# Front and projection stages of a four-layer kernel: inputs summed from plain loads, more statistics groups, normalisation moved to ScalarE, input stage reordered

## The reference, cut to what matters

```python
x = hidden_states                                   # (4, 1024, 256)
x = x + mamba(layernorm(x))                         # front + scan
x = x + top2_experts(layernorm(x))
x = x + attention(layernorm(x))                     # projection stage + attention
x = x + expert_choice(layernorm(x))

# mamba, up to its scan
xz = h @ in_proj_w;  x, z = split(xz)               # 256 -> 2 x 512
x = silu(conv4(x) + conv_b)
dt_low, B, C = split(x @ x_proj_w)                  # 64, 16, 16
dt = softplus(dt_low @ dt_proj_w + dt_bias);  du = dt * x

# attention, up to its scores
q = rope((h @ Wqa) @ Wqb);  k, v = split((h @ Wkva) @ Wkvb);  k = rope(k)
```

## Time and profile before

| | us |
|---|---|
| median of three runs | 2639.83 (2638.99 to 2640.31) |
| profiled execution, its own time | 2635.56 |
| span of that execution | 2633.9 |
| front stage | 0 to 235 |
| projection stage | 1381 to 1513 |

### The profile page before, as it was taken

The page is one execution under the profiler, slowest core; times in us unless marked ns, Lnnn a source line. Parts: engine busy times, 40 slices in busy tenths (PEclk is TensorE's granted clock), DMA queues, the critical chain, the costliest instruction groups (busy, mean ns, idle before and its releaser), DMA issues. The chain is left out here.

```text
span 2633.9 us, 35521 instructions
## 1 busy us (share of the span) xinstructions
PE 2274.5 (86%) x11483; PEld 1340.5 (51%) x11485; DVE 1810.7 (69%) x2771; ACT 1325.2 (50%) x2531; POOL 1337.9 (51%) x1000
## 2 busy tenths in 40 slices
PE   7994888989989986499985599999998539999998
PEld 3432444544545544399972334444445326666666
DVE  7997999999999995755544798888884651111200
ACT  4776888787887782022222546666665202111120
POOL 1545999899898891277755512222221012333332
PEclk9996999999999998699996889999999759999999
DMA  4457235124133104544437522112200322333322
GB/s 160 163 187 242 70 130 192 49 77 147 49 108 132 49 17 136 171 72 72 71 54 150 150 37 33 33 33 42 39 3 4 128 89 54 75 80 68 70 54 24
DMA packets 149650, 231.20 MB, mean 88 GB/s; under 512 B 26113, under 2 KB 98881, under 8 KB 149378
## 3 DMA queue, kind: packets, MB, share of 16 engines
q1 hardware_dynamic: 119170, 189.22, 23.2%
q0 software_dynamic: 30336, 40.16, 9.5%
HBM read 151.99 MB, written 81.66 MB: 89 GB/s over the span
## 5 line engine op out<-in xcount | busy, mean ns | idle before, releaser
L1114 POOL TENSOR_TENSOR scan_hC<-scan_h,scan_c_all 128x1024 f32<-128x1024 f32 x256 | 612.4, 2418 | 70.3 <-DVE scan_h L1034 69.2
L1034 DVE TENSOR_TENSOR_SCAN scan_h<-scan_dA,banks 128x1024 f32<-128x1024 f32 x224 | 504.3, 2275 | 22.9 <-ACT scan_dA L987 14.9
L884 PE MATMUL banks<-scan_hC,all_ident 128*128 128x512 f32 x1024 | 486.5, 600 | 26.4 <-DVE scan_xc L1041 26.4
L2200 ACT ACTIVATE attn_pt<-banks 128x1024 f32<-128x1024 f32 (+3 forms) x384 | 292.2, 810 | 186.9 <-PE banks L2147 185.7
L976 ACT ACTIVATE scan_scaled<-scan_duT,scan_bT 128x128 f32<-128x128 f32 x1024 | 312.0, 388 | 15.1 <-PE banks L861 14.7
L987 ACT ACTIVATE scan_dA<-scan_dt,mamba_a_neg 128x1024 f32<-128x1024 f32 x224 | 254.1, 1144 | 97.3 <-DVE scan_h L1034 96.9
L2084 POOL TENSOR_SCALAR_AFFINE_SELECT attn_pt<-attn_pt 128x256 f32<-128x256 f32 x256 | 103.5, 410 | 382.7 <-ACT attn_pt L2200 381.1
L2218 DVE TENSOR_REDUCE attn_m_lo<-banks 128x1 f32<-128x512 f32 (+3 forms) x432 | 266.8, 661 | 29.9 <-PE banks L2103 20.0
L884 PEld LDWEIGHTS banks<-scan_hC,all_ident 128*128 128x128 f32 x1024 | 185.2, 191 | 181.1 <-issue 130.6
L2874 DVE TENSOR_TENSOR ffn_y<-banks,ffn_gates 128x512 f32<-128x512 f32 x32 | 22.1, 691 | 357.1 <-PE banks L2773 350.4
L2710 POOL DMA_INDIRECT out<-ffn_y,ffn_ids x64 | 101.0, 1577 | 297.8 <-DVE ffn_y L2874 288.1
(11 more groups left out here) (320 smaller groups left out, 3742.1 us busy)
## 6 DMA issues: line engine op xcount, KB each, us to landing
scan_c_all<-scratch_bc SPq DMA_DIRECT2D x64, 512.0 KB, 6.3
ffn_w<-in_e_w SPq DMA_DIRECT2D x16, 1024.0 KB, 5.2
attn_Q<-scratch_q SPq DMA_DIRECT2D x96, 128.0 KB, 4.1
scratch_x<-front_xc SPq DMA_DIRECT2D x8, 1024.0 KB, 4.3
scratch_z<-front_zs SPq DMA_DIRECT2D x8, 1024.0 KB, 6.5
scratch_dt<-front_lw SPq DMA_DIRECT2D x8, 1024.0 KB, 4.1
scratch_du<-front_du SPq DMA_DIRECT2D x8, 1024.0 KB, 4.4
scan_dt<-scratch_dt SPq DMA_DIRECT2D x16, 512.0 KB, 3.5
```

The source lines that it names most:

```text
L884: mm = pe.matmul(PS[:, YB + i, :], ident[:, :], hC[:, u % NHC, i * BANK:(i + 1) * BANK], start=s == 0, stop=s == NST - 1, skip_group_check ...
L1034: dve.tensor_tensor_scan(h[:, u % NH, :], decay, drive, 0.0, ALU.mult, ALU.add).then_inc(scanned, 1)
L1114: pool.tensor_tensor(hC[:, u % NHC, :], h[:, u % NH, :], c_all[:, s, :], ALU.mult).then_inc(hC_done, 1)
L2200: act.activation(pt[:, at % 4, 2 * pair:2 * pair + 2, 0:width], PS[:, ST + 2 * pair:ST + 2 * pair + 2, 0:width], ACT.Exp, scale=HD ** -0.5 ...
```

## The change

In `norm_front`: ScalarE copies one x group ahead of the exponential and the three others behind it; the square root comes after all four; the logarithms come after the turned copy; the last z and conv SiLUs alternate. VectorE makes the first convolution ahead of the softplus terms, and takes the turned copy directly behind them. The last chunk's dt and du are made by VectorE alone, ahead of the last split, and stored in two halves.

In `norm_project`: chunks 0 and 1 are loaded even and odd by plain DMAs (odd rows into the buffer `rq`), and VectorE adds them. There are six statistics groups, and each chain is cut at the square root (`chain_to_var`, `chain_to_nmr`) and placed by `STATS_AT` and `STD_AT`. From chunk 2 on ScalarE normalises all four tiles (`ON_ACT = 4`), between its low copy and its row copy; GpSimd normalises chunk 1. TensorE makes the low projection ahead of turning rows. Loads of chunks 4 to 7 wait for the sum two chunks back.

```diff
@@ norm_front, SP
+                    else:
+                        for m in range(0, MT, 2):
+                            sp.wait_ge(last_dt, m + 2)
+                            sp.dma_start(chunk_of("dt", c)[:, m:m + 2, :], lw[:, m:m + 2, :]).then_inc(out_dt, 16)
+                            sp.wait_ge(last_du, m + 2)
+                            sp.dma_start(chunk_of("du", c)[:, m:m + 2, :], du[:, m:m + 2, :]).then_inc(out_du, 16)
@@ norm_front, ScalarE
             for q in STEPS:
+                if head(q):
+                    copy_x(q, 0)
                 if tail(q):
+                    exps(q - 2)
                 if head(q):
-                    for m in range(2):
+                    for m in range(1, MT):
                         copy_x(q, m)
                 if 0 < q < len(GROUPS):
                     std(q)
...
                 if head(q + 1):
                     copy_turned(q + 1)
+                if tail(q):
+                    logs(q - 2)
@@ norm_front, VectorE
             for q in STEPS:
+                if head(q):
+                    convolve(q, 0)
                 if tail(q):
                     softplus_terms(q - 2)
+                    if head(q + 1):
+                        copy_turned(q + 1)
                 if head(q):
-                    for m in range(MT):
+                    for m in range(1, MT):
                         convolve(q, m)
...
-                if mid(q):
+                if mid(q) and head(q):
                     split_bc(q - 1)
             c = NCH - 1
-            for m in range(LAST_DVE):
+            dve.wait_ge(out_dt, 16 * c)
+            dve.wait_ge(out_du, 16 * c)
+            for m in range(MT):
                 dve.wait_ge(ln_done, MT * c + m + 1)
                 dve.wait_ge(less_done, MT * c + m + 1)
                 dve.tensor_tensor(lw[:, m, :], lw[:, m, :], less[:, m, :], ALU.subtract).then_inc(last_dt, 1)
-            dve.wait_ge(out_du, 16 * c)
-            for m in range(LAST_DVE):
                 dve.wait_ge(last_dt, m + 1)
                 dve.tensor_tensor(du[:, m, :], lw[:, m, :], xc[:, c % XS, m, :], ALU.mult).then_inc(last_du, 1)
+            split_bc(c)
@@ norm_project
-        GROUPS = [(0, 1), (1, 2), (2, 4), (4, 6), (6, NCH)]
+        GROUPS = [(0, 1), (1, 2), (2, 3), (3, 4), (4, 6), (6, NCH)]
+        ON_ACT = 4
+        STD_AT = {0: 2, 1: 3, 2: 4, 4: 5}
+        STATS_AT = {0: 3, 1: 4, 3: 5}
@@ norm_project, SP
+            for c in range(2):
+                load_x(c)
+                sp.dma_start(odd_rows(c), odd[:, c * TC:(c + 1) * TC, :]).then_inc(odd_in[c], 16)
+            load_x(2)
             loads.start(sp)
-            for c in range(2, NCH):
-                if c >= 4:
-                    sp.wait_ge(x_added[c - 4], 16)
+            load_x(3)
+            for c in range(4, NCH):
+                sp.wait_ge(x_added[c - 2], 16)
                 load_x(c)
@@ norm_project, TensorE
                 if q:
                     turn_heads(q - 1)
+                if q + 1 < NCH:
+                    project_low(q + 1)
                 if q + 2 < NCH:
                     turn_rows(q + 2)
-                if q + 1 < NCH:
-                    project_low(q + 1)
@@ norm_project, ScalarE
+            def normalise(c):
+                group = next(k for k, (first, last) in enumerate(GROUPS) if first <= c < last)
+                act.wait_ge(small, CHAIN * (group + 1))
+                act.wait_ge(xn_psum, 2 * (c - 1))
+                for i in range(ON_ACT):
+                    tile = c * TC + i
+                    act.activation(xn[:, c % 2, i, :], X[:, tile, :], ACT.Identity, scale=rstd[:, tile:tile + 1],
+                                   bias=nmr[:, tile:tile + 1]).then_inc(norm_act, 1)
...
                 if q < NCH:
                     copy_up(q)
+                if q in STD_AT:
+                    std(STD_AT[q])
                 if q:
                     first_part(q - 1)
-                if q + 2 < NCH:
-                    copy_rows(q + 2)
                 if q + 1 < NCH:
                     copy_low(q + 1)
-                if q in (0, 2):
-                    std(3 + q // 2)
+                if q + 2 < NCH:
+                    normalise(q + 2)
+                    copy_rows(q + 2)
                 if q:
                     second_part(q - 1)
@@ norm_project, VectorE, in the statistics chain and in the steps
+                    if c < 2:
+                        dve.wait_ge(x_in[c], 16)
+                        dve.wait_ge(odd_in[c], 16)
+                        at_rows = slice(c * TC, (c + 1) * TC)
+                        dve.tensor_tensor(X[:, at_rows, :], X[:, at_rows, :], odd_rows(c), ALU.add).then_inc(odd_added, 1)
...
                 if q < NCH:
-                    rope(q)
-                if q in (0, 2):
-                    chain(3 + q // 2)
+                    by_cos(q)
+                if q in STD_AT:
+                    chain_to_nmr(STD_AT[q])
+                if q < NCH:
+                    join(q)
+                if q in STATS_AT:
+                    chain_to_var(STATS_AT[q])
@@ norm_project, GpSimd
-            add_odd(0)
-            add_odd(1)
             pool.memset(heads[1][KR:KM, :, :], 1.0).then_inc(k_set, 1)
             pool.wait_ge(k_set, 1)
             add_odd(2)
-            normalise(1)
             add_odd(3)
-            normalise(2)
-            add_odd(4)
+            normalise(1, 0)
             loads.wait(pool)
             for q in range(NCH):
                 turn(q)
                 if q < 2:
+                    add_odd(4 + 2 * q)
                     add_odd(5 + 2 * q)
-                if q + 3 < NCH:
-                    normalise(q + 3)
-                if q == 0:
-                    add_odd(6)
```

100 lines of the change are left out of this document (54 added, 46 removed).

## The result

The changed kernel takes 2630.60 us (median of 7 runs, 2626.39 to 2632.03), the kernel before, on the same chip, 2638.99 (7 runs): a ratio of 0.9966, 95% interval 0.9956 to 0.9975, 8.4 us less. Forecast were 2642.3 in a range of 2631 to 2652: the time lies just under the range, and the sign is the other one.

What follows compares the result with a forecast made beforehand. VectorE was taken to bound the front, a chain of waits the projection stage. Front -0.5 plus projection +3 (opening and step 1 -13.6, steps 2 to 5 +14.2, end +2.8) gave +2.5: 2642.3 us, range 2631 to 2652.

Steps and rivals of the forecast that it cites:

- (b): Front, ScalarE's step: TensorE waits for z banks, clock falls, x projection 6.0 us, ScalarE's step 22.9 (20.3 to 24).
- (f): Projection stage, opening: up copies start at 1405.2 instead of 1415.16, 10.0 us earlier; chunk 3's even load lands at 1399.5.
- (g): Projection stage, steps: ScalarE's tiles on the chain and the low clock make a step 13.4 us (11.1 to 15.3).
- (a): Front: one convolution ahead of the softplus terms removes VectorE's 1.27 us of idleness, making its step 22.0.
- (c): Front: GpSimd's products run into VectorE's splits, +1.0 us per split (0 to +3.8), VectorE's step 23.0.
- (d): Front, early steps: square roots come after four copies; the first costs +3.5 us, net +2.1 into the later steps.
- (e): Front, tail: last chunk's products all on VectorE, du of chunk 6 issued earlier; -2.1 us (0 to -3.5).
- 1.0 of it the same wait: Projection stage, step 1 of 14.4 us: 1.0 is tiles waiting for the statistics behind the cosine product.
- R1: Rival, chance 0.22: the high clock holds, projection steps 2 to 5 take 11.1 us, front loops 22.4; kernel 2629.
- R2: Rival, chance 0.18: ScalarE's tiles on the projection chain at the low clock throughout, 15.3 us a step; kernel 2651.
- R3: Rival, chance 0.10: GpSimd's products run over the front's splits, each step 24.1 us instead of 23.3; kernel 2646.
- R4: Rival, chance 0.08: projection opening fails, chunk 3 at 1403 or later, +4 to +5 us; kernel 2647.

Runs made afterwards that it cites:

- e1: The kernel before with only the front stage of the change: 2635.97 us, -3.5 against the kernel before.
- e2: The kernel before with only the projection stage of the change: 2634.87 us, -4.6 against the kernel before.
- e8: The changed kernel with VectorE's softplus terms ahead of the first convolution again: 2640.62 us, +2.0 against the kernel before.
- e15: The changed kernel with one of the input projection's two contraction blocks left out: -12.2 us against the kernel before; stage behind the front starts at 227.57.
- e16: The kernel before with one of the input projection's two contraction blocks left out: -6.3 us against the kernel before; stage behind the front starts at 228.14.
- e14: The changed kernel with three and four idle matmuls ahead of the front's last x and dt projections: 2626.97 us, -12.2 against the kernel before.
- e12: The changed kernel with GpSimd's tiles of chunk 1 ahead of chunk 3's adding DMA: 2629.55 us, -8.1 against the kernel before.
- e4: The changed kernel with the statistics' reciprocal and product ahead of the cosine product on VectorE: 2619.85 us, -19.6 against the kernel before.

## Why the prediction was wrong, step by step

The forecast erred by 3.0 us in the front and by 7.6 in the projection stage, by the medians of e1 and e2. Three terms were wrong: the matmul group in (b), the opening in (f) and the end in (g).

(a) Right. VectorE's idle 1.27 went, the first later step is 22.00, and e8 puts the order's worth at 1.71 a step.

(b) This is the step that failed in the front: "three matmul groups of 0.85". A group is two contraction blocks, each of two records of 0.43: 1.72. The rows of before show it, since the earlier trace rows has eight records in 3.60, and an x projection has four contraction blocks. With 0.85 the "some 10 us of each step" look thin; with 1.72 TensorE works through them, and it is busy for 94.6% of the stretch. The x projection took 3.64, not 6.0, and ScalarE's step stayed under VectorE's. With groups made as short as that (e15, e16) the x projections took 5.3 to 6.7 as forecast, and the change brought the front 0.57 us, beside the 0.5 forecast. That agreement is luck. By the prediction's terms it is -2.3 in the five steps (-0.8 forecast), +1.6 ahead of them (+2.1) and +0.2 in the tail (-2.1); and the second half of (b), that ScalarE's longer step would then hold VectorE, failed as well. With the group right the five steps gained 5.3, with it halved 2.3: the misread number cost 3.0 us there, and the other 1.5 of the steps' error was in (b)'s ScalarE step and (c)'s disturbance. Mended by these 3.0, the forecast would have gone from +2.5 to -0.5; the larger error is in (f) and (g).

The Trainium skill (FP8 and Floating Point Precision, section TensorE Precision Notes) says that a full fp32 product takes four passes. By it a block of 512 columns is 4 x 512 / 2.4 GHz = 0.85 and a group of two blocks 1.71, an estimate; the trace agrees (1.76 in the row at 83.44). Beside the count of blocks it would have caught the slip.

(c) Right in kind: the splits at 84.72, 106.72 and 129.57 run beside GpSimd's work, and the steps that they open are 22.00, 22.85 and 22.58, against 21.92 behind the one at 152.15 (the last step, 21.33, has no turned copy in it): +0.1, +0.9 and +0.7 for the +1.0 taken. The rule cited with it from the Trainium skill (GPSIMD Engine Reference, section 1. Specifications: GpSimd's way to SBUF is shared with VectorE) came out at +3.8 for a split wholly beside a product; no split of the changed kernel was. In e15 one began beside a product: its subtraction took 1.64, the trace agrees, and the split 4.85 (101.47 to 106.32) for 2.73.

(d) The first root: wait 4.22, VectorE goes on at 38.61, +1.8 against the +3.5 forecast; the second at 61.42 against 62.1. The later steps begin +1.1 late (84.72 against 83.59), forecast +2.1; over all profiles of this code they begin at 84.7 to 86.3, and without the change at 82.7 and 83.6, so +2.1 was a fair size.

(e) The tail gave 0.46 (34.71 from the last split's start to the next stage, before 35.17), forecast 2.1. In this profile x projection and dt projection took 5.37 and 7.06 at the lower clock; in ten others of the same tail it was 33.4 to 34.9 long, and before the change 35.17 and 36.23 (e2). So 0.3 to 2.8 us are gained, the forecast lies within, and one profile can't judge it. With both at full speed (e14) it is 33.12, and it hangs on the landing of du, as forecast.

Front: -4.66 against -0.5, of which (a), (b) and (c) are -5.3 (five steps, 116.01 less 110.68) for the -0.8 forecast, (d) +1.1 and (e) -0.5.

(f) This step failed too, in size: the opening came 3.75 earlier than forecast, 19.95 after the stage's start for 23.7 (19.6 to 20.8 over all profiles of it). Chunk 3's even load landed 14.6 after the start, for the 18.0 that I took by adding loads up in SP's order. What the sum lacks the traces show: an adding DMA holds the DMA engines longer than a plain one. In the opening before (1376 to 1402) GpSimd's adding DMAs moved 1.69 MB in 43.8% of the 16 engines' time and SP's plain ones 2.99 MB in 42.5%, 1.8 times as long per MB; after, 1.05 MB took 28.1% and 4.48 MB 58.4%, 2.1 times. Up to the landing that GpSimd waits for, 207 GB/s were moved before (1381.50 to 1396.30) and 243 after (1378.00 to 1392.70). No run takes this singly. Nor does moving that load help: in e12 GpSimd's tiles no longer wait for it, and the low projection at the lower clock, which ends close by, holds the opening.

(g) The mechanism held in part: tiles of 2.08 are on the chain, and the low clock comes behind TensorE's idle time. But the sum has it in each of steps 2 to 5, and their heads took 1.90, 2.76, 1.47 and 2.77: step 4, with heads at full speed, is as long because its tiles waited 1.81 for the statistics. That the four add up to the forecast is in part luck. Step 0 was 10.44 (10.3 forecast), steps 2 to 5 56.02 (55.6), step 1 13.21 (14.4). Off were step 6 and the end together, 27.95 for 31.0: without tiles the copies and heads were at full speed again. So the stage's error is 3.75 in (f), 1.2 in step 1 and 3.05 at the end, less 0.4 and 0.1; the 1.2 is this profile's, since step 1 took 14.1 to 15.1 in the six others. The term at the end that failed is "up copies and heads at the low clock, +2.5". What (g) did not see is that its "1.0 of it the same wait" was the cheapest thing to remove (e4) and set off part of the low clock.

Of the rivals none came true: R1's number, 2629, is near, but its reason is wrong, since the clock did not hold in the projection steps (0.77 over the stage, up tiles of 2.93) and had never been at risk in the front. R2 had 15.3 a step, and 13.4 to 14.8 were measured. R3's splits of 5 us did not come (2.7 to 3.7 before the tail). R4 is excluded by the opening. The range was said to reach down to R1's price, which is 2629, and was then given from 2631; the measured 2630.60 lies between the two. A range down to 2629 would have held it, but by luck, since R1's reason failed.

Open: whether the adding DMAs are the whole of (f)'s error, what decides whether the clock falls in steps 3 and 5, and what idle work is worth there. The front's 4.7 us in the profile and 3.5 in e1's medians differ by less than the untouched stages do from profile to profile.

## What to carry to other kernels

Before a clock argument is made, count the records of one matmul group in the trace and add up the engine's work over one step: here 21.5 of 22 us, and the argument was over. Then ask whether the slower engine would set the pace at all: with TensorE made thin, it did not. Waits for two tiny instructions can cost more than their length where TensorE's idle time brings the lower clock behind it (5.8 us of waits, 9.1 us of steps); look at what stands in front of them on their engine. Profile the same code more than once before a difference of 1 or 2 us is given a cause. Idle work that is to keep a clock has to be sized from the records (each of these matmuls left two) and tried: in the front's tail it brought 0.3 to 1.8 us, in the projection steps nothing once the wait itself was gone.

## Unexpected about the hardware

GpSimd's normalisation of a tile (256 columns) took 0.54 us alone and 1.5 beside VectorE's products of two SBUF inputs (6.02 for four), nearly three times as long. And one projection stage, in the same code, took 124.2 to 128.7 us in seven profiles: its steps 3 and 5 alone took 11.05 in one of them and up to 13.9 in others, where heads and up tiles ran at half the speed. In e4 four steps in a row have the same idle time of 1.80 ahead of the up tiles, and the heads behind it took 2.70, 1.48, 2.77 and 1.48 (from 1431.70 on).
